# A fused decoder layer: the routed expert rows in 24 blocks of two 64-row halves instead of 31 blocks of 128 rows

## What is computed

```
logits = einsum('th,eh->te', x, gate_w)                  # 1024 tokens, 16 experts
topk_w, topk_idx = top_k(softmax(logits), 2)
gu = einsum('th,ehj->etj', x, w_gate_up)                 # 256 -> 2 x 176
h  = silu(gu[..., :176]) * gu[..., 176:]
y  = einsum('eti,eih,te->th', h, w_down, combine)        # 176 -> 256, weights of the top 2
y += shared expert of width 352 on every token
```

## Time and profile before

| what | us |
|---|---|
| median of 3 runs (252.64 to 252.76) | 252.67 |
| the profiled execution's own time | 252.71 |
| its span in the profile | 250.7 |
| first `expert_up` to last `expert_down` on TensorE | 77.2 |
| TensorE busy in the whole span | 237.4 (95%) |
| GpSimd busy in the whole span | 92.5 (37%) |

### The profile page before, as it was taken

The page is one execution under the profiler, slowest core; times in us unless marked ns, Lnnn a source line. Parts: engine busy times, 40 slices in busy tenths (PEclk is TensorE's granted clock), DMA queues, the critical chain, the costliest instruction groups (busy, mean ns, idle before and its releaser), DMA issues.

```text
span 250.7 us, 5232 instructions
## 1 busy us (share of the span) xinstructions
PE 237.4 (95%) x1660; PEld 177.2 (71%) x1660; DVE 148.5 (59%) x452; ACT 129.3 (52%) x465; POOL 92.5 (37%) x110
## 2 busy tenths in 40 slices
PE   8969799999999999999999999799999999999995
PEld 6635475666766677898788787567777777777784
DVE  1568888887889856437896588653223232323184
ACT  2146988989889898540524216124343434343440
POOL 2111211112111100102662004655777777777460
PEclk9999999999999999999999999999999999999999
DMA  7999877100005400006013000222333333343495
GB/s 217 267 366 387 283 174 171 53 3 3 3 0 160 171 3 3 1 3 229 1 41 129 0 3 4 63 68 81 105 105 107 105 95 112 89 102 111 144 338 188
DMA packets 20388, 28.10 MB, mean 112 GB/s; under 512 B 2369, under 2 KB 17355, under 8 KB 20363
## 3 DMA queue, kind: packets, MB, share of 16 engines
q1 hardware_dynamic: 16683, 19.01, 24.5%
q0 software_dynamic: 2976, 8.13, 11.0%
q10 hardware_dynamic: 704, 0.64, 0.8%
HBM read 21.61 MB, written 6.16 MB: 111 GB/s over the span
## 4 chain that ended last, share of the span: by engine, by line
PE 71%; ACT 13%; DVE 8%; issue 4%; DMA 1%; POOL 1%; ACTq 0%; POOLq 0%; DVEq 0%
PE bank L898 15%; PE bank L910 11%; ACT pr_s L1010 10%; PE bank L829 8%; PE bank L531 5%; PE bank L573 4%; PE bank L560 3%; PE bank L879 3%; PE bank L889 3%; PE bank L658 2%; PE bank L536 2%; PE bank L623 2%; PE bank L649 1%; PE bank L668 1%; DMA qx_s<-ffn_in,prT 1%
## 5 line engine op out<-in xcount | busy, mean ns | idle before, releaser
L1010 ACT ACTIVATE pr_s<-bank,mx 128x128 f32<-128x128 f32 x128 | 45.2, 383 | 8.0 <-DVE mx L1236 8.0
L898 PE MATMUL bank<-gu_s,bxT 128*128 x124 | 41.7, 460 | 0.2 <-DVE bxT L1561 0.2
L1567 DVE TENSOR_TENSOR pr_s<-bank,pr_s 128x176 f32<-128x176 f32 x31 | 10.6, 341 | 51.6 <-ACT pr_s L1165 50.9
L492 POOL DMA_INDIRECT expert_out<-by,prT x31 | 31.0, 1000 | 14.8 <-ACT by L1000 7.5
L487 POOL DMA_INDIRECT qx_s<-ffn_in,prT x31 | 30.1, 972 | 14.6 <-issue 8.2
L1000 ACT ACTIVATE prT<-bank 128x512 f32<-128x512 f32 (+1 forms) x63 | 31.1, 497 | 2.9 <-PE bank L573 1.8
L910 PE MATMUL bank<-dn_s,prT 88*128 x124 | 31.7, 379 | 0.0
L1010 ACT ACTIVATION_READ_ACCUMULATOR pr_s<-bank,mx 128x1 f32 x128 | 28.6, 224 | 0.0
L898 PEld LDWEIGHTS bank<-gu_s,bxT 128*128 128x128 f32 x124 | 21.2, 190 | 7.2 <-issue 0.4
L1000 ACT ACTIVATE by<-bank 128x256 f32<-128x256 f32 x31 | 11.9, 383 | 23.5 <-PE bank L910 21.9
L1236 DVE TENSOR_REDUCE mx<-bank 128x4 f32<-128x512 f32 x32 | 20.5, 683 | 4.7 <-PE bank L560 4.7
(11 more groups left out here) (194 smaller groups left out, 438.2 us busy)
## 6 DMA issues: line engine op xcount, KB each, us to landing
gu_s<-in_w_gu SPq DMA_DIRECT2D x8, 704.0 KB, 7.0
dn_s<-in_w_dn SPq DMA_DIRECT2D x4, 704.0 KB
gu_s<-in_ctx_in SPq DMA_DIRECT2D x2, 512.0 KB, 9.2
ffn_in<-x_s SPq DMA_DIRECT2D x4, 256.0 KB, 2.4
cv_s<-expert_out SPq DMA_DIRECT2D x4, 256.0 KB, 4.1
x_s<-expert_out SPq DMA_DIRECT2D x4, 256.0 KB, 5.7
out<-x_s SPq DMA_DIRECT2D x7, 128.0 KB, 3.6
gu_s<-in_x_t SPq DMA_DIRECT2D x1, 768.0 KB, 10.7
```

The costliest lines, as they stand in the source:

```text
L492: pool.indirect_dma_start(expert_out[:], bass.IndirectOffsetOnAxis(ap=idx[:, 1, k:k + 1], axis=0), by[:, k % RB, :], None).then_inc(dma_sc ...
L898: last = mm(bank[2 + i % 2][:, 0:2 * I], bxT[:, i % 2, k, :], gu_s[:, k, bass.ds(e, 1), :], start=k == 0, stop=k == KD - 1)
L1010: last = nc.scalar.activation(pr_s[:, n % 2, h, :], score_bank(n)[:, h * T:(h + 1) * T], ACT.Exp, bias=mx[:, n % 4, h:h + 1], accum_out=de ...
```

## The change

Half blocks: a block has two halves of 64 rows (`HT`), and each half may belong to another expert. An expert's first 64 pairs have a fixed place, the upper half (rows 64 to 127) of block e, for e = 0 to 15. All further pairs go to at most 32 "more" halves (`MORE`), numbered through the experts: the lower halves of blocks 0 to 15 hold one each, and blocks 16 to 23 two each. So `BLOCKS` is 24. With the counts above 26 "more" halves hold pairs, so that block 20 is the last with pairs.

On TensorE a block's `expert_up` and `expert_down` become two products each, of 64 rows, one into partitions 0 to 63 and one into 64 to 127 of the same bank. The lower half reads the weights of the expert in the register, as before. The upper half of blocks 0 to 15 reads expert i. Blocks 16 to 23 have a second run-time expert, whose weights SP loads from HBM into one of four places (`SB`): `gu_x` (360,448 bytes) and `dn_x` (180,224 bytes), in the memory of tiles that only the first stages use. `w_gu` and `w_dn` are laid out per partition in HBM for that. The numbers that are printed below are of the changed kernel where it is named.

```diff
-BLOCKS = (SLOTS + E * (T - 1)) // T
+HT = T // 2
+MORE = 2 * ((SLOTS - 1) // HT // 2 + 1)
+BLOCKS = E + (MORE - E) // 2
...
+SB = 4
...
+def more_of(i):
+    return i if i < E else E + 2 * (i - E)
...
+            sp.wait_ge(dve_block_experts, 1)
+            for j in range(BLOCKS - E):
+                d = more_of(E + j) + 1
+                e = sp.value_load(bei[0:1, d:d + 1], min_val=0, max_val=E - 1)
+                if j >= SB:
+                    sp.wait_ge(pe_expert_down, E + j - SB + 1)
+                sp.dma_start(gu_x[:, j % SB], w_gu[bass.ds(e, 1), :, :, :].rearrange("e p k n -> p (e k) n")).then_inc(dma_staged[j % SB], 16)
+                sp.dma_start(dn_x[:, j % SB], w_dn[bass.ds(e, 1), :, :, :].rearrange("e p k n -> p (e k) n")).then_inc(dma_staged[j % SB], 16)
             sp.wait_ge(dve_ring, 1)
...
             def expert_up(i):
...
+                if i >= E:
+                    pe.wait_ge(dma_staged[(i - E) % SB], 32 * ((i - E) // SB + 1))
                 for k in range(KD):
-                    last = mm(bank[2 + i % 2][:, 0:2 * I], bxT[:, i % 2, k, :], gu_s[:, k, bass.ds(e, 1), :],
-                              start=k == 0, stop=k == KD - 1)
+                    mm(bank[2 + i % 2][0:HT, 0:2 * I], bxT[:, i % 2, k, 0:HT], gu_s[:, k, bass.ds(e, 1), :],
+                       start=k == 0, stop=k == KD - 1, skip_group_check=True)
+                    last = mm(bank[2 + i % 2][HT:T, 0:2 * I], bxT[:, i % 2, k, HT:T],
+                              gu_s[:, k, i, :] if i < E else gu_x[:, (i - E) % SB, k, :],
+                              start=k == 0, stop=k == KD - 1, skip_group_check=True)
```

More of the change, by code:

```diff
@@ L13 @@
+import math
 import numpy as np
@@ L85, in routing_constants @@
     p = np.arange(128)[:, None]
-    c[:, R_THR:R_THR + B] = 128.0 * np.arange(B)
+    c[:, R_THR:R_THR + THRESHOLDS] = HT * (1.0 + np.arange(THRESHOLDS))
     c[:, R_LOW:R_LOW + E * E] = (np.arange(E)[None, :] < np.arange(E)[:, None]).reshape(1, -1)
-    c[:, R_BLK:R_BLK + BLOCKS] = np.arange(BLOCKS)
-    c[:, R_SLOT:R_SLOT + T] = np.arange(T)
+    lower = [E + more_of(i) for i in range(BLOCKS)]
+    upper = [i if i < E else E + more_of(i) + 1 for i in range(BLOCKS)]
+    c[:, R_BLK:R_BLK + HALVES] = lower + upper
+    c[:, R_SLOT:R_SLOT + HT] = np.arange(HT)
+    c[:, R_MORE:R_MORE + MORE] = np.arange(MORE)
+    c[:, R_BASE:R_BASE + E] = E * HT - HT - HT * np.arange(E)
     c[:, R_TOK:R_TOK + B] = T * np.arange(B)
     c[:, R_TOK + B:R_TOK + 2 * B] = p + 1
-    c[:, R_RING:R_RING + RB] = RB - 1 - np.arange(RB)
+    c[:, R_RING:R_RING + RB] = E + 1 + 2 * (RB - 1 - np.arange(RB))
+    c[:, R_RING + RB:R_RING + 2 * RB] = 2 * E + 2 * (RB - 1 - np.arange(RB))
     c[:, R_DUMMY:R_DUMMY + BLOCKS] = DUMMY + T * np.arange(BLOCKS) + p + 1
@@ L167, in decoder_layer @@
         den = sb("den", [128, 2, H])
-        oT = sb("oT", [128, 2, KD, T])
-        xb = sb("xb", [128, 2, D])
+        oT = first_half(2, KD, T)
+        xb = first_half(2, D)
+        staged = early[0][:, 0:SB * (KD * 2 * I + 2 * D)].rearrange("p (r n) -> p r n", r=SB)
+        gu_x = staged[:, :, 0:KD * 2 * I].rearrange("p r (k n) -> p r k n", k=KD)
+        dn_x = staged[0:IH, :, KD * 2 * I:].rearrange("p r (k n) -> p r k n", k=2)
         bxT = sb("bxT", [128, 2, KD, T])
@@ L255, in decoder_layer @@
         dve_ring = sem("dve_ring")
+        dma_staged = [sem(f"dma_staged{i}") for i in range(SB)]
         dve_first_sum, dve_second_sum, dma_out = sem("dve_first_sum"), sem("dve_second_sum"), sem("dma_out")
@@ L867, in slot_table @@
                         for f in range(2):
-                            last = mm(bank[4][:, k * BLOCKS:(k + 1) * BLOCKS], hot[:, k * B + t, :],
-                                      num_b[:, f, k * B + t, :], start=t == 0 and f == 0, stop=t == B - 1 and f == 1)
+                            for u in range(2):
+                                last = mm(bank[4][u * HT:(u + 1) * HT, k * BLOCKS:(k + 1) * BLOCKS], hot[:, k * B + t, :],
+                                          num_b[:, f, k * B + t, u * BLOCKS:(u + 1) * BLOCKS],
+                                          start=t == 0 and f == 0, stop=t == B - 1 and f == 1, skip_group_check=True)
                 last.then_inc(pe_slot_table, 1)
@@ L909, in expert_down @@
                 for k in range(2):
-                    last = mm(bank[4 + i % 2][:, 0:D], bhT[:, i % 2, k, :], dn_s[:, k, bass.ds(e, 1), :],
-                              start=k == 0, stop=k == 1)
+                    mm(bank[4 + i % 2][0:HT, 0:D], bhT[:, i % 2, k, 0:HT], dn_s[:, k, bass.ds(e, 1), :],
+                       start=k == 0, stop=k == 1, skip_group_check=True)
+                    last = mm(bank[4 + i % 2][HT:T, 0:D], bhT[:, i % 2, k, HT:T],
+                              dn_s[:, k, i, :] if i < E else dn_x[:, (i - E) % SB, k, :],
+                              start=k == 0, stop=k == 1, skip_group_check=True)
                 last.then_inc(pe_expert_down, 1)
```

100 lines of the change are left out of this document (58 added, 42 removed).

## The result

The changed kernel takes 279.44 us (median of 4 runs, 278.68 to 280.19); the kernel before, beside it, 252.71 us (252.64 to 253.08). The ratio is 1.105 (95% interval 1.102 to 1.109): 10.5% slower. The forecast was 270.7 us in a range of 259 to 284. The profiled execution takes 279.82 us, 278.0 of it the span.

The account below looks back on a forecast made before the run. TensorE was taken to bound the loop, with the results' path also setting the end. Span 250.7 + 1.5 (routing) + 10.6 (loop: -17.4 + 13.6 + 14.4) + 5.9 (end) = 268.7, so 270.7 us of time, range 259 to 284.

Parts of the forecast that it names:

- my main case: Whole kernel: the summed forecast without a fall of the clock, 268.7 us of span and 270.7 us of time, given 0.50.
- the first rival: TensorE's clock falls to 1.2 GHz around the four waits: 8.2 us more there, about 1 at the end; 280 us, chance 0.27.
- Fewer blocks, whole overlap: Loop: 24 blocks instead of 31, both halves running at once at a whole block's price; 17.4 us less.
- Going in and out of half width: Loop: 44 half-width stretches between full-width transposes, 0.31 us each; 13.6 us more, bounds 4 to 20.
- The waits: Before expert_up of blocks 20 to 23: bare weight transfers, 3.6 us more each; 14.4 in all, bounds 10.4 to 19.2.
- The clock: TensorE around the four waits: the summed forecast included no fall from the full 2.4 GHz.
- Routing: Before the loop: products end 0.6 us later, slot table 0.7 longer, 0.15 going out; loop starts 1.5 us later (0 to 5).
- The end: After the loop: the results' path alone sets the end, 14.8 us in place of 8.9; 5.9 more (3 to 7).

Follow-up runs that it names:

- fill: Changed kernel with 16 unneeded matmuls of 128 columns put before expert_up's wait for the transfer in blocks 20 to 23; 271.85 us.
- after_again: The changed kernel, unchanged, measured once more on the third occasion; 279.30 us.
- split: Changed kernel with up and down weights of blocks 20 to 23 released and awaited separately, each with its own semaphore; 256.24 us, then 257.27 on another occasion.
- split_wide: split with expert_up and expert_down as full-width matmuls, all rows taking the lower half's expert; 252.81 us on the first occasion.
- split_paired: split with both transposes ahead of both products in TensorE's order, so one half-width stretch per iteration; 255.00 us.
- spread: split_paired_tail with the first four groups of staged loads issued one by one after expert_up of blocks 4, 6, 8 and 10; 251.78 us.
- split_again: split, unchanged, measured once more on the third occasion; 257.27 us, ratio 0.978 to a kernel before that was again near 263.
- fill_tailfill: fill with 20 more unneeded matmuls between the last part's first and second product group at the end; 271.89 us.
- split_wide_again: split_wide, unchanged, measured once more on the second occasion; 246.73 us, ratio 0.976 to the kernel before.
- split_paired_tail: split_paired with both last shared-expert products moved ahead of the weighing in VectorE's order; 250.81 us, ratio 0.990 to the kernel before.

## Why the prediction was right, and where it was not

The direction and the range were right, and so was the mechanism but for the clock. The number was not that of my main case: the outcome is the first rival, "the clock falls", given 0.27 and 280 us; measured 279.44. The range was drawn to take that rival in; the main sum alone missed by 8.7 us. By the steps, in us of span (forecast 268.7, measured 278.0):

- **Fewer blocks, whole overlap:** right. Pairs of records begin together, and 352 columns of a pair cost 0.29 + 0.29, as one full-width matmul did.
- **Going in and out of half width:** right, a little high. 0.285 a stretch in place of 0.31 makes 12.5 in place of 13.6, 1.1 less. The price read from 32-row matmuls carries over to 64 rows. The Trainium skill (TensorEngine Tiling (Array Packing), Key Properties) says that a change of tiling mode drains TensorE; the trace agrees in that each change costs time, 0.15 us on the way in and 0.13 to 0.15 out. What the engine does in that time isn't shown.
- **The waits:** right. From `expert_down` to the matmul 4.1 was forecast; 4.2, 4.3, 4.2 and 4.3 were measured. The loads land 3.8 to 3.9 us after the first issue (223.23 to 227.01 the first time), for which I had 3.8. The 3.2 us that follow from the fit in the Trainium skill (DMA: Bandwidth & Descriptors, Anatomy of one DMA), which is for GpSimd's path, would have been 0.5 to 0.7 short here, each time.
- **The clock:** this step failed. "No row of before shows a fall, for or against" was true, and I then took the level that it had as the likelier one. From `expert_down(16)` to `expert_down(20)` the forecast comes to 25.8 (two iterations of 3.11, two of 2.58 without a `block_transpose` and with one stretch, and 14.4 for the waits); 34.7 was measured, 8.9 more. The four waits are 0.6 of that (17.0 for 16.4); the work between them took 17.7 where it takes 10.0 in `fill`, so the clock is 7.7 (medians: 279.44 - 271.85 = 7.6; the rival had 8.2). The last 0.6 is work that is longer than its pieces even at full clock, such as 0.51 for the first one after a wait. The Trainium skill (TensorE: Matmul & The Clock Gate, HAM oscillation) describes this alternation of short work and waits for transfers, with the clock at half rate again after every wait; the trace agrees, with 0.50 in most of the work.
- **Routing:** right, with a term too high. The products end at 154.92 (forecast 154.9; DVE's five pieces add up to 1.0 us and not 1.1, which changes nothing behind them). The slot table takes 1.20 in place of 0.97, so 0.2 more and not 0.7, which its 64 matmuls of 24 columns can do only if they overlap at least in part. The first `expert_up` begins at 165.77 in the chain, 1.2 later than before and 0.3 earlier than forecast. The gathers beside the staged loads cost next to nothing in this trace (0.5 us of TensorE's waits, where before has 0.3), but 1.1 us in the trace of `after_again` and up to 1.4 in those of faster kernels, so "nothing" was too low.
- **The end:** 20.25 after block 20's `expert_down`, for 18.5 forecast. 0.9 of it is the clock (forecast about 1, but only in the rival); about as much is left, and the last result load landing after 6.3 us, where the earlier trace rows had at most 5.9, is the only thing I see for it.

Sum: 268.7 - 0.3 (first `expert_up`) - 1.1 (from there to `expert_down(16)`) + 8.9 + 1.8 (the end) = 278.0. Of the whole loss of 26.7 us, `split` removes 22 to 23 by releasing and awaiting four loads elsewhere, and what remains comes from the edges of half width (12.5) and the end, now in the open, which seven fewer blocks (17.4) don't quite pay for. From the loop's end on it is 16.7 us in place of 8.9 (20.25 less the 3.6 us of loop behind block 20's `expert_down`), and the first `expert_up` comes 1.2 later: 12.5 + 7.8 + 1.2 - 17.4 = +4.1, and `split` is at 256.2 to 257.3 where 252.7 + 4.1 is 256.8.

What stays open: why the kernel before takes 263 us on some occasions. It isn't the granted clock, as one such run had 1.00 and took 262.21. In the three kernels with an iteration below 3 us (`split_wide`, `split_paired`, `spread`) the traces of those occasions show ScalarE standing still, mostly for 1 to 4 us at a time, with no releaser on the core (VectorE only twice, 0.8 us each, in `split_wide`). The traces of `split`, `split_again`, `fill`, `fill_tailfill` and `after_again` from the same occasions have no such pause, nor has any of the second occasion. Loads on the queues of kind "instruction" don't explain them by their timing: the trace of `split_wide_again` has them in the loop as well and no pause, and that of `split_wide` has no such load between 190 and 210 us, where three of the four pauses of its chain lie. That these pauses are also what costs the kernel before 10 us was not shown.

## What to carry to other kernels

When a buffer is refilled for block i+4 by what block i releases, look at which instruction releases it and which one waits: here one semaphore for two loads, released at the end of an iteration, left 4 us bare, and releasing each load by its own last reader and waiting for it at its own use hid all of it. Price a wait on TensorE twice, once as the wait and once as the granted clock in the work behind it, above all where waits and short work alternate. And before moving an instruction to the head of an in-order queue, list what then stands behind it and what that ran beside until now.

## What the hardware showed that I had not expected

- A single wait of 4 us after 52 us of full work was followed by 1.2 GHz in place of 2.4. In the work between the second and the third wait (4.3 us, which take 2.8 in `fill`) the clock came back only towards the end (0.63 on the mean of 236.7 to 241.2), and behind the next wait it was at 0.50 again.
- 64 matmuls that compute nothing make the program 7.6 us faster.
- The slowest gather of token rows beside four groups of staged loads landed after 5.8 to 7.9 us by the chains, where the traces of the kernel before have at most 3.4 in that stretch. TensorE's waits for gathers there took 0 to 1.4 us, with no order by kernel: 0.5 and 1.1 in two traces of the changed kernel, 0 in `split` and `fill`, 1.3 and 1.4 in `split_wide_again` and `split_paired_tail`.
- The pauses of ScalarE of 1 to 4 us, on some occasions and in the kernels with a short iteration only, with no releaser on the core. Their cause is open.
